# Both transposed slots of a substep in a row, in a graph attention kernel: a change of the order in which TensorE is given its work

## The reference

```python
h = jnp.maximum(_layernorm(x, axis=-1), 0.0)
adj = jnp.maximum(adjacency_matrix, eye)
q = jnp.einsum('nd,hdk->hnk', h, Wqs)          # keys k and values v in the same way
scores = jnp.einsum('hqk,hmk->hqm', q, k) * kd ** (-0.5)
scores = scores + IDENTITY_BIAS * eye - MASK_VAL * (1.0 - adj)
att = jax.nn.softmax(scores, axis=-1)
return x + jnp.einsum('hqm,hmk,hko->qo', att, v, Wo)
```

## Time and profile before

| | |
|---|---|
| time, median of 3 runs | 3127.39 us (3122.81 to 3129.61) |
| span of the profiled execution | 3131.2 us |
| TensorE busy | 3056.8 us, 98% |
| VectorE busy | 2444.3 us, 78% |
| ScalarE busy | 2171.6 us, 69% |
| GpSimd busy | 492.8 us, 16% |
| granted TensorE clock, mean | 0.992 of full speed |

### The profile page before, as it was taken

How to read it: one execution, slowest core, us unless ns; L and a number is a source line. 1 busy time by engine, 2 the same in 40 slices (tenths; PEclk the granted TensorE clock), 3 DMA queues, 4 the chain that set the end, 5 groups by cost and what they waited for, 6 DMA issues and landing times.

```text
span 3131.2 us, 58791 instructions
## 1 busy us (share of the span) xinstructions
PE 3056.8 (98%) x18368; PEld 1892.8 (60%) x18368; DVE 2444.3 (78%) x4345; ACT 2171.6 (69%) x3297; POOL 492.8 (16%) x658
## 2 busy tenths in 40 slices
PE   7999999999999999999989999999999999999998
PEld 5566666666666666666556655666665666565664
DVE  6778788887878887887557877878877778777775
ACT  3677777777777777777547767767777667677675
POOL 3011111101111110111001111111111111111110
PEclk9999999999999999999999999999999999999999
DMA  5234444433444443344424433444433444433442
GB/s 154 53 85 88 95 79 98 84 81 78 91 91 84 94 85 85 73 95 87 94 74 80 88 84 73 87 93 81 93 79 72 86 94 81 93 79 72 89 93 52
DMA packets 217847, 267.82 MB, mean 86 GB/s; under 512 B 57472, under 2 KB 176768, under 8 KB 217728
## 3 DMA queue, kind: packets, MB, share of 16 engines
q1 hardware_dynamic: 173568, 178.51, 24.6%
q0 software_dynamic: 41984, 83.91, 16.1%
q10 hardware_dynamic: 2176, 4.19, 0.4%
HBM read 169.87 MB, written 12.71 MB: 58 GB/s over the span
## 4 chain that ended last, share of the span: by engine, by line
PE 92%; DVE 3%; issue 3%; DMA 1%; SPq 1%; DVEq 0%; ACT 0%; POOL 0%; POOLq 0%
PE psS L383 31%; PE psO L406 23%; PE psT L396 21%; PE psO L417 10%; PE psP L368 2%; PE psS L341 2%; DVE S L631 1%; PE psP L426 1%; PE psO L356 1%; PE psP L356 1%; DVE PT L645 1%; DMA S<-in_x 1%; SPq L239 0%; DMA S<-hT_scratch 0%; PE psT L327 0%
## 5 line engine op out<-in xcount | busy, mean ns | idle before, releaser
L631 DVE CUSTOM_DVE_ANT_0 S<-psS,B 128x1024 f32<-128x1024 f32 x1024 | 1239.6, 1211 | 169.0 <-PE psS L383 151.5
L517 ACT ACTIVATE S<-S,negm 128x1536 f32<-128x1536 f32 (+1 forms) x768 | 1094.8, 1427 | 62.9 <-DVE negm L638 59.7
L524 ACT ACTIVATE PT<-psT 128x512 f32<-128x512 f32 x768 | 457.0, 595 | 656.0 <-PE psT L396 654.3
L406 PE MATMUL psO<-PT,V 128*64 128x256 f32 x5120 | 836.0, 405 | 0.0
L396 PE MATMUL psT<-ident,S 128*128 128x128 f32 x5120 | 797.6, 283 | 31.4 <-DVE PT L645 24.3
L396 PEld LDWEIGHTS psT<-ident,S 128*128 128x128 f32 x5120 | 566.2, 141 | 398.2 <-issue 293.6
L383 PE MATMUL psS<-K,QH 128*128 128x512 f32 x2048 | 738.3, 442 | 8.4 <-DVE mx L631 5.9
L383 PE MATMUL psS<-K,QL 128*128 128x512 f32 x2048 | 643.8, 395 | 0.0
L645 DVE COPY PT<-psT 128x512 f32<-128x512 f32 x512 | 352.7, 689 | 332.4 <-PE psT L396 292.1
L658 DVE STREAM_TRANSPOSE S<-S 128x1536 f32<-128x1536 f32 x256 | 454.0, 1773 | 38.0 <-PE psO L417 37.9
L406 PEld LDWEIGHTS psO<-PT,V 128*64 128x64 f32 x5120 | 254.1, 135 | 362.4 <-issue 248.6
(11 more groups left out here) (52 smaller groups left out, 1056.1 us busy)
## 6 DMA issues: line engine op xcount, KB each, us to landing
S<-S SPq DMA_DIRECT2D x1536, 96.0 KB, 2.2
B<-in_adj POOLq DMA_DIRECT2D x256, 256.0 KB, 5.4
hq<-hT_scratch SPq DMA_DIRECT2D x32, 256.0 KB, 3.2
RB<-rden_scratch SPq DMA_DIRECT2D x128, 64.0 KB, 3.2
S<-in_x SPq DMA_DIRECT2D x8, 512.0 KB, 3.6
hT_scratch<-S ACTq DMA_DIRECT2D x8, 512.0 KB, 4.1
acc<-in_x POOLq DMA_DIRECT2D x16, 256.0 KB, 4.5
partial_scratch<-res POOLq DMA_DIRECT2D x16, 256.0 KB, 3.2
```

The costliest lines, as they stand in the source:

```text
L406: last = nc.tensor.matmul(psO[a * KD:(a + 1) * KD, 0:QW], V[:, 2 * s + a, h * KD:(h + 1) * KD], PT[:, s % RING, a * QW:(a + 1) * QW], star ...
L517: nc.scalar.activation(part, part, ACT.Exp, bias=negm[:, h % 2, q:q + 1], accum_out=sums[:, h % 2, q, e:e + 1]).then_inc(probs_ready, 1)
L524: nc.scalar.activation(PT[:, s % RING, :], psT[s % 2][:, :], ACT.Copy).then_inc(pt_act, 1)
L631: nc.vector.tensor_tensor_reduce(out=part, in0=psS[j % 2][:, :], in1=B[:, q, k * SLOT:(k + 1) * SLOT], scale=SCALE, scalar=LOWEST, op0=ALU ...
```

## The change

In each substep TensorE now makes T(2c) and T(2c+1) one after the other, then S(c+2) (and P), and then V(2c-2) and V(2c-1) one after the other. The programs of the other engines, the waits of each operation, and the tail of the step are as before.

```diff
             for c in range(SUBSTEPS):
                 transposes(i, h, 2 * c)
+                transposes(i, h, 2 * c + 1)
                 if nxt:
                     scores(i1, h1, c + 2)
                 if prev and h % 2 == 0 and c == PROJECT_AT:
...
                     project(*last_step(i, h))
                 if c:
                     values(i, h, 2 * c - 2)
-                transposes(i, h, 2 * c + 1)
-                if c:
                     values(i, h, 2 * c - 1)
```

## The result

The changed kernel takes 3183.53 us (median of 4 runs, 3180.72 to 3184.13); the kernel before took 3128.19 us in 4 runs. The ratio is 1.0176, with a 95% interval of 1.0162 to 1.0191: slower by 55 us, where 52 us were forecast (3179 us).

The account below looks back on a forecast made before the run. TensorE was taken as the bound, apart from 24.3 us of waits for VectorE's copy. Order terms 3 + 5 + 6 + 17 + 8 + 1 - 1.5 = +38.5 us, clock +13, together +52 on 3127.4: 3179 us, range 3128 to 3215.

Parts of the forecast that it names:

- h = 1, 32: Steps with h = 1: T(4) 1.03 us late, less 0.93 us won in substeps 2 to 4; +3 us in all.
- h = 2, 32: Steps with h = 2, P between S(3) and V(0): +0.2 us each, +6 us in all.
- h = 0, in time, 17: Steps with h = 0 without a late take(1): T(4) 1.26 us late, less 0.93; +5 us in all.
- The gain: Each substep with c = 2 to 4: two fewer edges of V, 2.96 us in place of 3.27, 0.31 us less.
- The wait: Substep 1, h = 1: T(3), moved forward, waits for VectorE's take(1), so TensorE stands for 1.26 us.
- The late steps: Second group, 13 steps with h = 0 where VectorE stops before take(1): +17 us for order, +13 us for 8 clock drops.
- The slightly late steps at h = 3: take(1) ends 0.3 to 0.8 us later in 18 of 30 steps: +8 us; the other 12 steps +1 us.
- The full gain: Rival: take(1) in time, substep 1 wins 0.31 us too, 154 us less in 124 steps: 2973 us; chance 5%.
- VectorE's stops: Rival: the new order frees the second group's 13 stops, late steps lose waits and clock drops: 3124 us; chance 16%.
- the last rival: Rival: each of 124 ordinary waits at T(3) brings a 1.6 us clock drop, +198 us: 3377 us; chance 6%.
- One premise: TensorE's clock falls by wait length at T(3): five of six waits over 1.7 us, none of 1.6 or less.

Follow-up runs that it names:

- the pair of kernels without the loop: VectorE's second group written out without a loop: on the changed kernel 3121.8 us, on the kernel before 3101.43 us.
- the combined kernel: Changed kernel with T(3) behind S(3) and P in substep 1, take(1) ahead of sum_halves at h = 1 and 3, VectorE's second group without a loop: 2974.07 us.

## Why the prediction was right

Its steps, against the distances from VL to VL in the two profiles:

| steps | forecast each | measured each | measured in all |
|---|---|---|---|
| h = 1, 32 | +0.10 | +0.14 | +5 us |
| h = 2, 32 | +0.2 | +0.26 | +8 us |
| h = 0, in time, 17 | +0.33 | +0.25 to +0.41 | +6 us |
| h = 0, late, 13 | +1.29, and 1.6 for 8 clock drops | +0.7 to +4.4, mean +2.46 | +32 us |
| h = 3, 30 | +0.42 (18) or +0.10 (12) | -0.35 to +0.63 | +3 us |

*The gain.* A substep was put at 2.96 us and takes 2.96 to 2.97, and the runs with pairs in substeps 2 to 4 alone price it at 103 us in all. The reason given for it, the change of width, stood the test of the full-width V. The price of 0.15 us rests on the trace alone. The 0.31 us were a hundredth or two too much each, which is the 0.04 us by which a step at h = 1 came out dearer than forecast.

*The wait.* T(3) was put at 7.24 us behind VL and came at 7.22 (680.52 - 673.30). The profile shows the 1.26 us from T(3)'s due start as 1.11 us of idle time behind T(2) at h = 1, and as 1.23 to 1.37 us at h = 2 and 0. Moving take(1) ahead shortened the 1.11 to 0.33 us, so it is VectorE's order that sets it, and not T(1) or ScalarE.

*The late steps.* Mechanism and sign were right, and the size nearly: 17 and 13 us were forecast, 32 measured by the distances, 36 by the pair of kernels without the loop. The clock did fall in all 13, but in four of them it stayed down twice as long as in the others (6.8 us against 3.4).

*The slightly late steps at h = 3* are the term that was mis-sized: +9 us were forecast, +3 came. In the profile before, take(1) was 0.3 us late or more in 17 of the 30 (the prediction counts 18); in the profile after, in only 3. The multiplication ahead of it (line 675) took up to 1.26 us in the profile before and up to 0.95 after, in place of 0.42, where it was late. What it collides with wasn't tried, and whether the longer step has moved it is not shown.

*A term left out.* The sum has no entry for the first step of each group. From its T(0) to its VL it takes 22.1 and 23.4 us before and 19.6 and 20.4 us after, 2.5 and 3.0 us less. No sum_halves stands ahead of take(1) there, and T(3) doesn't wait, so the pairs win without a loss. Four pairs at 0.31 us would make 1.2 us of each. The rest isn't explained, but for the clock in the second group, which was low for 3.4 us of that step in place of 6.8. The other steps add up to 53 us with the last ones of each group. The profiled spans differ by only 48 us, because of these 5.5 us and of small differences, +1.3 to -0.5 us, ahead of the groups and behind them.

That the medians, 55 us apart, came so near to the 52 forecast is in part luck: the late steps cost 2 us more than forecast, the steps with h = 3 cost 6 us less, and the first steps, left out, won 5.5.

The rivals. The full gain would have needed take(1) 1.26 us earlier; with the wait out of the way the combined kernel gained 152 us, of which about 26 are VectorE's stops. VectorE's stops didn't go away with the new order. The clock didn't fall in ordinary steps, whose wait of 1.1 to 1.4 us is shorter than any at T after which it fell in a step here, nor in the three steps with h = 3 whose T(3) waited 1.6 to 1.7 us, which the upper end of the range had allowed for. (It is this rival, and not the one that stands last, that "the last rival" under the clock means.)

One premise is weaker than the prediction took it to be. It goes by the length of the wait, and over all kernels the length alone doesn't decide: the clock fell after a wait of 1.64 us with pairs in substeps 2 to 4, and stayed at 2.4 GHz after six waits of 2.6 to 2.8 us with take(1) ahead of sum_halves. The two readings that the sum needed held all the same: no drop after a wait of 1.4 us, and one after each wait of 4 us.

## What to carry to other kernels

An order that saves switches on the busiest engine is worth what each switch costs, but read for every block that is moved forward what it waits for and what covered that wait: here 0.3 us were won in each of three substeps and 1.0 to 1.3 us lost in a fourth, by one wait that had been covered with 0.3 us to spare. Apply such a rule where there is slack and leave it where there is none: the same pairs in three substeps alone made the kernel 3% faster, where in all they made it 2% slower. And look at what an engine does behind a loop's jump: a stop there is cheap or dear according to who waits for the first thing behind it.

## What the runs showed of the hardware

- A change between matmuls of 64 columns on alternate halves of the array and full ones costs TensorE about 0.15 us each way in float32. With V made full width, T between two V took the 0.44 us that it takes in a row of T.
- VectorE stops for 2.6 to 3.2 us behind each of the 13 jumps back of its loop in the second group, and then for 0.3 to 1.3 us once more a few instructions later; packets of its instruction queue start at the same places. In the first group, where that queue moves nothing during the loop, a jump costs 0.12 us. Written out, the 64 steps ran without these stops.
- TensorE's clock fell to 1.2 GHz after five of six waits of 1.7 to 1.9 us at T(3) in the kernel before and after none of 1.6 us or less there. In the late steps of three other kernels it fell after 12 of 13 waits of 2.1 to 2.5 us (only V in pairs), 7 of 13 of 2.6 to 3.3 us (take(1) ahead of sum_halves), and 13 of 13 of 3.8 to 4.3 us (after the change). The length of a wait alone doesn't decide it.
